# Slot tables of their own for the two batch entries, and the token chain's last norm on ScalarE, in a one-core vision block

## The reference

```python
# token stage: three 5-row convolutions over tokens x joints, a layer norm before each and one behind
h = layernorm(x, ln0_g, ln0_b); h = relu(conv2d(h, conv1_w, conv1_b, ((2, 2), (1, 1))))
h = layernorm(h, ln0_g, ln0_b); h = relu(conv2d(h, conv2_w, conv2_b, ((2, 2), (0, 0))))
h = layernorm(h, ln1_g, ln1_b); h = relu(conv2d(h, conv3_w, conv3_b, ((2, 2), (0, 0))))
h = layernorm(concat(h[:, :t], h[:, t:]), ln1_g, ln1_b) @ out_w + out_b
# attention with L1 distances, 8 heads of 64, a zero score added to each softmax
a[s, t, head] = -sum_w |q[s, head, w] - k[t, head, w]| / 8
a = softmax(concat(a, 0), axis=s)[:, :t]
o = sum over heads of (a applied to vf, and a transposed applied to vb)
h = h + x' + (o * sigmoid(1.702 * o)) @ fanin_w.T + fanin_b      # x' = layernorm(h)
# 32 experts, one chosen per token by argmax of x'' @ router_w.T
h = h + x'' + relu(relu(x'' @ W1[e] + b1[e]) @ W2[e] + b2[e])     # x'' = layernorm(h)
```

## Time and profile before

| | us |
|---|---|
| median of 3 runs | 3578.32 |
| lowest and highest | 3576.53, 3587.60 |
| the profiled execution's own time | 3586.24 |
| its span, first to last instruction | 3584.1 |

### The profile page before, as it was taken

How to read it: one execution, slowest core, us unless ns; L and a number is a source line. 1 busy time by engine, 2 the same in 40 slices (tenths; PEclk the granted TensorE clock), 3 DMA queues, 4 the chain that set the end, 5 groups by cost and what they waited for, 6 DMA issues and landing times. The chain is left out here.

```text
span 3584.1 us, 78481 instructions
## 1 busy us (share of the span) xinstructions
PE 3276.2 (91%) x23008; PEld 2420.3 (68%) x23008; DVE 3115.8 (87%) x4449; ACT 2694.5 (75%) x4801; POOL 2851.3 (80%) x2724
## 2 busy tenths in 40 slices
PE   5899999999999999999999999999999999999886
PEld 4666667666667766667666677666677666677554
DVE  3889988898898898888899899899899899898884
ACT  1777877777877777777777777777777777777774
POOL 1788888888888888878888888888888888888874
PEclk8999999999999999999999999999999999999998
DMA  3777877787777787777887777787877787777874
GB/s 94 154 157 153 161 151 154 150 165 154 156 153 156 153 162 156 155 148 151 158 160 155 157 153 154 157 158 155 159 153 155 156 158 155 155 153 152 160 157 82
DMA packets 198692, 545.31 MB, mean 152 GB/s; under 512 B 68054, under 2 KB 132438, under 8 KB 145272
## 3 DMA queue, kind: packets, MB, share of 16 engines
q0 software_dynamic: 73728, 503.35, 71.0%
q1 hardware_dynamic: 124920, 41.40, 5.9%
HBM read 10.79 MB, written 2.10 MB: 4 GB/s over the span
## 5 line engine op out<-in xcount | busy, mean ns | idle before, releaser
L805 DVE TENSOR_REDUCE S<-psU 128x16 f32<-128x1024 f32 x2176 | 2603.5, 1217 | 295.7 <-PE psU L403 288.4
L403 PE MATMUL psU<-flat,kT 99*128 99x256 bf16 x16384 | 2315.7, 275 | 230.5 <-ACT absd L601 106.6
L601 ACT ACTIVATE absd<-psU 128x1024 f32<-128x1024 f32 x1920 | 1957.8, 1023 | 627.0 <-PE psU L403 604.7
L403 PEld LDWEIGHTS psU<-flat,kT 99*128 99x128 bf16 x16384 | 1489.2, 98 | 915.2 <-DVE S L805 235.7
L1072 POOL TENSOR_TENSOR absd<-absd 128x1024 f32<-128x1024 f32 (+2 forms) x512 | 1182.1, 2309 | 195.3 <-DMA absd<-absd 194.3
L1061 POOL DMA_DIRECT2D absd<-absd x512 | 453.9, 886 | 297.6 <-ACT absd L601 254.5
L1076 POOL TENSOR_TENSOR absd<-absd 128x512 f32<-128x512 f32 (+2 forms) x512 | 611.0, 1193 | 40.2
L1079 POOL TENSOR_TENSOR absd<-absd 128x256 f32<-128x256 f32 (+2 forms) x512 | 352.4, 688 | 40.1
L415 PE MATMUL psC<-c1in,w 128*128 128x384 f32 (+1 forms) x930 | 315.1, 421 | 0.6
L501 PE MATMUL psZ<-P,v 128*128 128x256 f32 x1024 | 311.2, 386 | 0.8 <-ACT P L719 0.8
L434 PE MATMUL psC<-c3in,w 128*128 128x128 f32 x1240 | 255.6, 289 | 4.5 <-DVE c3in L847 4.2
(11 more groups left out here) (166 smaller groups left out, 2187.0 us busy)
## 6 DMA issues: line engine op xcount, KB each, us to landing
absd<-absd POOLq DMA_DIRECT2D x416, 1024.0 KB, 7.8
flat<-qparts SPq DMA_DIRECT2D x3072, 8.0 KB, 4.0
absd<-absd POOLq DMA_DIRECT2D x64, 768.0 KB, 6.5
absd<-absd POOLq DMA_DIRECT2D x32, 512.0 KB, 4.8
xin<-in_x SPq DMA_DIRECT2D x32, 192.0 KB, 7.9
flat<-pattern SPq DMA_DIRECT2D x4, 768.0 KB, 10.8
out_h<-result SPq DMA_DIRECT2D x32, 64.0 KB, 5.9
w<-in_w SPq DMA_DIRECT2D x1, 1280.0 KB
```

Of the source, the lines that this page charges most:

```text
L403: mm = nc.tensor.matmul(psU[:, slot % PLACES, m], kT[0:ROWS + 3, b, m, :], flat[0:ROWS + 3, half % HALVES, :, lo:lo + BLOCK], start=True, ...
L601: nc.scalar.activation(absd[:, c % GROUPS, :, u], psU[:, slot % PLACES].rearrange("p (n a) s w -> p n (a s w)", n=2), ACT.Abs).then_inc(a_ ...
L805: nc.vector.tensor_reduce(S[:, b, hd, SB * c:SB * c + SB], psU[:, slot % PLACES].rearrange("p a s w -> p s a w"), AX.XY, ALU.add, apply_ab ...
```

## The change

Three things are done. SHARED changes in two chunks: the third one's heads for ScalarE are (1, 2, 3, 4) instead of (0, 2, 4, 6), the fifteenth one's (2, 4, 6) instead of (0, 3, 6); the number of slices for each engine stays the same. LAST_AFTER goes from 17 to 21, and the tables KQ_AT and AT_AT become pairs of tables, one for each batch entry, with nearly all entries of all tables chosen anew; where the code read AT_AT["x"] it now reads AT_AT[b]["x"]. And the last norm of the token chain is applied on ScalarE as scale * x + bias, for which GpSimd makes the bias -mean * rstd by two more instructions (shift) behind the root, instead of VectorE's (x - mean) * rstd.

```diff
-SHARED = [(0, 2, 4, 6), (0, 2, 4, 6), (0, 2, 4, 6), (0, 2, 4, 6), (1, 3, 5), (0, 2, 4, 6), (0, 2, 4, 6), (0, 2, 4, 6),
-          (0, 2, 4, 6), (0, 2, 4, 6), (0, 2, 4, 6), (3, 6), (0, 2, 4, 6), (0, 2, 4, 6), (0, 3, 6), (0, 2, 4, 6)]
+SHARED = [(0, 2, 4, 6), (0, 2, 4, 6), (1, 2, 3, 4), (0, 2, 4, 6), (1, 3, 5), (0, 2, 4, 6), (0, 2, 4, 6), (0, 2, 4, 6),
+          (0, 2, 4, 6), (0, 2, 4, 6), (0, 2, 4, 6), (3, 6), (0, 2, 4, 6), (0, 2, 4, 6), (2, 4, 6), (0, 2, 4, 6)]
-LAST_AFTER = 17
+LAST_AFTER = 21
-TOK_ACT = Steps("copy relu1 relu2 relu3a relu3b turned")
+TOK_ACT = Steps("copy relu1 relu2 relu3a relu3b norm0 norm1 turned")
-TOK_DVE = Steps("".join(LN.format(x) + LN_APPLY.format(x) for x in "abc") + LN.format("d") + "norm0 norm1 h")
-TOK_POOL = Steps("vara rstda varb rstdb varc rstdc vard rstdd")
+TOK_DVE = Steps("".join(LN.format(x) + LN_APPLY.format(x) for x in "abc") + LN.format("d") + "h")
+TOK_POOL = Steps("vara rstda varb rstdb varc rstdc vard rstdd meand shiftd")
-KQ_AT = dict(kT=21, q=13, q_len=1, qpart1=13, qrest1=14, qpart2=38, qpart3=37)
-AT_AT = dict(vf=0, vb=7, v_len=0, turn_len=0, exp=20, exp_len=8, rden=27, scale=30, scale_len=8, turna=42, turnb=45,
-             pv=47, pv_len=8, half=52, sum=53, tanh=54, gate=58)
+KQ0 = dict(kT=22, q=13, q_len=0, qpart1=12, qrest1=13, qpart2=29, qpart3=37)
+KQ1 = dict(kT=15, q=11, q_len=1, qpart1=11, qrest1=13, qpart2=35, qpart3=32)
+KQ_AT = (KQ0, KQ1)
+AT0 = dict(vf=1, vb=7, v_len=0, turn_len=1, exp=20, exp_len=11, rden=32, scale=34, scale_len=7, turna=42, turnb=45,
+           pv=47, pv_len=7, half=52, sum=53, tanh=54, gate=55)
+AT1 = dict(vf=3, vb=6, v_len=0, turn_len=0, exp=20, exp_len=5, rden=27, scale=29, scale_len=13, turna=42, turnb=45,
+           pv=47, pv_len=5, half=52, sum=53, tanh=55, gate=56)
+AT_AT = (AT0, AT1)
-EX_AT = dict(fan=60, h2=59, rstd=58, x=67, turn=70, route=75, pick=76, turnoh=82, hida=84, hidb=86, hid_len=0, out=90,
-             out_len=4, back=105)
-NORM_AT = dict(stat=4, rstd=2, x=6, turn=38, part1=28, rest1=28, part2=32, part3=31, hx=89)
-HAND_AT = dict(xT=12, hx=65)
-TOK_AT = dict(copy=0, a=10, conv1=21, len1=22, b=45, conv2=55, len2=10, c=65, conv3=75, len3=32, d=108, turn=122,
-              out=126, root=0, gap=7)
+EX_AT = dict(fan=60, h2=59, rstd=64, x=67, turn=69, route=75, pick=75, turnoh=82, hida=85, hidb=87, hid_len=0, out=91,
+             out_len=5, back=105)
+NORM_AT = dict(stat=4, rstd=4, x=6, turn=36, part1=29, rest1=26, part2=33, part3=34, hx=87)
+HAND_AT = dict(xT=6, hx=89)
+TOK_AT = dict(copy=0, a=10, conv1=21, len1=22, b=44, conv2=55, len2=10, c=65, conv3=75, len3=30, d=108, turn=122,
+              out=125, root=0, gap=6)
...
                 if slot == TOK_AT["turn"]:
-                    pe.wait_ge(by_dve, TOK_DVE.after(q, "norm1"))
+                    pe.wait_ge(by_act, TOK_ACT.after(q, "norm1"))
...
+                if slot == TOK_AT["d"] + TOK_AT["gap"]:
+                    act.wait_ge(by_pool, TOK_POOL.after(q, "shiftd"))
...
+                    for b in range(2):
+                        nc.scalar.activation(resn[:, b, :], z[:, b * 2 * J:(b + 1) * 2 * J], ACT.Identity,
+                                             bias=nmr["d"][:, b:b + 1], scale=rstd["d"][:, b:b + 1]).then_inc(by_act, 1)
...
-                if slot == TOK_AT["d"] + TOK_AT["gap"]:
-                    dve.wait_ge(by_pool, TOK_POOL.after(q, "rstdd"))
-                    lead("turn")
-                    for b in range(2):
-                        nc.vector.tensor_scalar(resn[:, b, :], rows(2 * J)[:, b, :], mv["d"][:, b, 0:1],
-                                                rstd["d"][:, b:b + 1], ALU.subtract, ALU.mult).then_inc(by_dve, 1)
...
+                        if name == "d":
+                            shift("d", by_pool, lambda s: TOK_POOL.after(q, s + "d"))
```

More of the change, by code:

```diff
@@ L190, in vit_tower @@
         rstd = {k: sb("rstd" + k, [T, 2]) for k in "abcdne"}
-        mr = {k: sb("mr" + k, [T, 2]) for k in "ne"}
-        nmr = {k: sb("nmr" + k, [T, 2]) for k in "ne"}
+        mr = {k: sb("mr" + k, [T, 2]) for k in "dne"}
+        nmr = {k: sb("nmr" + k, [T, 2]) for k in "dne"}
         h = sb("h", [T, 2, LAT])
@@ L459, in kq @@
                 g = 2 * p + b
-                if slot == KQ_AT["kT"]:
+                if slot == KQ_AT[b]["kT"]:
                     take_bank(keys_act, K_ACT.after(g, "kT"))
@@ L467, in kq @@
                     mm.then_inc(keys_pe, 1)
-                for m in spread(slot, KQ_AT["q"], KQ_AT["q_len"], 2):
+                for m in spread(slot, KQ_AT[b]["q"], KQ_AT[b]["q_len"], 2):
                     if m == 0:
@@ L479, in attend @@
                 for n, name in enumerate(("vf", "vb")):
-                    for m in spread(slot, AT_AT[name], AT_AT["v_len"], 2):
+                    for m in spread(slot, AT_AT[b][name], AT_AT[b]["v_len"], 2):
                         if m == 0:
@@ L489, in attend @@
                 for n, name in enumerate(("turna", "turnb")):
-                    for m in spread(slot, AT_AT[name], AT_AT["turn_len"], 4):
+                    for m in spread(slot, AT_AT[b][name], AT_AT[b]["turn_len"], 4):
                         if m == 0:
@@ L496, in attend @@
                             mm.then_inc(at_pe, 1)
-                for n in spread(slot, AT_AT["pv"], AT_AT["pv_len"], HEADS):
+                for n in spread(slot, AT_AT[b]["pv"], AT_AT[b]["pv_len"], HEADS):
                     if n == 0:
@@ L624, in tok @@
                         nc.scalar.activation(y, y, ACT.Relu, bias=b3[:, hf:hf + 1]).then_inc(by_act, 1)
+                if slot == TOK_AT["d"] + TOK_AT["gap"]:
+                    act.wait_ge(by_pool, TOK_POOL.after(q, "shiftd"))
+                    if isinstance(p, int) and p == 1:
+                        act.wait_ge(lead_pe, TOK_PE.after(0, "turn"))
+                    for b in range(2):
+                        nc.scalar.activation(resn[:, b, :], z[:, b * 2 * J:(b + 1) * 2 * J], ACT.Identity,
+                                             bias=nmr["d"][:, b:b + 1], scale=rstd["d"][:, b:b + 1]).then_inc(by_act, 1)
                 if slot == TOK_AT["turn"] + 1:
@@ L678, in kq @@
                 g = 2 * p + b
-                if slot == KQ_AT["kT"] + 1:
+                if slot == KQ_AT[b]["kT"] + 1:
                     act.wait_ge(keys_pe, K_PE.after(g, "kT"))
@@ L685, in kq @@
                                          psZb[0:ROWS, 0:BLOCKS * T], ACT.Copy).then_inc(keys_act, 1)
[L686 removed]
+                if slot == KQ_AT[b]["qpart1"]:
                     act.wait_ge(queries_pe, Q_PE.after(g, "q"))
@@ L699, in attend @@
                 for n, name in enumerate(("vf", "vb")):
-                    if slot == AT_AT[name] + AT_AT["v_len"]:
+                    if slot == AT_AT[b][name] + AT_AT[b]["v_len"]:
                         act.wait_ge(at_pe, AT_PE.after(g, name))
@@ L703, in attend @@
                                              ACT.Copy).then_inc(at_act, 1)
-                for n in spread(slot, AT_AT["exp"], AT_AT["exp_len"], HEADS):
+                for n in spread(slot, AT_AT[b]["exp"], AT_AT[b]["exp_len"], HEADS):
                     if n == 0:
@@ L711, in attend @@
                                          accum_out=den[:, n:n + 1]).then_inc(at_act, 1)
-                for n in spread(slot, AT_AT["scale"], AT_AT["scale_len"], HEADS):
+                for n in spread(slot, AT_AT[b]["scale"], AT_AT[b]["scale_len"], HEADS):
                     if n == 0:
@@ L720, in attend @@
                                              psZ[:, :].rearrange("p (h t) -> p h t", h=4), ACT.Copy).then_inc(at_act, 1)
-                if slot == AT_AT["half"]:
+                if slot == AT_AT[b]["half"]:
                     act.wait_ge(at_pe, AT_PE.after(g, "pv"))
@@ L907, in kq @@
                 g = 2 * p + b
-                if slot == KQ_AT["qrest1"]:
+                if slot == KQ_AT[b]["qrest1"]:
                     dve.wait_ge(queries_act, Q_ACT.after(g, "qpart1"))
@@ L916, in attend @@
                 g = 2 * p + b
-                if slot == AT_AT["rden"]:
+                if slot == AT_AT[b]["rden"]:
                     dve.wait_ge(at_act, AT_ACT.after(g, "exp7"))
                     nc.vector.reciprocal(rden[:, :], den[:, :]).then_inc(at_dve, 1)
-                if slot == AT_AT["sum"]:
+                if slot == AT_AT[b]["sum"]:
                     dve.wait_ge(at_act, AT_ACT.after(g, "half"))
@@ L923, in attend @@
                         .then_inc(at_dve, 1)
-                if slot == AT_AT["gate"]:
+                if slot == AT_AT[b]["gate"]:
                     dve.wait_ge(at_act, AT_ACT.after(g, "tanh"))
@@ L1134, in kq @@
                 g = 2 * p + b
-                if slot == KQ_AT["qpart3"]:
+                if slot == KQ_AT[b]["qpart3"]:
                     pool.wait_ge(queries_act, Q_ACT.after(g, "qpart2"))
```

15 lines of the change are left out of this document (9 added, 6 removed).

## The result

The changed kernel takes 3792.98 us (median of six runs, 3788.12 to 3799.30) where the kernel before takes 3578.71 us (six runs, 3571.75 to 3587.60): 1.0595 times as long, 95% interval 1.0579 to 1.0611. The forecast was 3505, the range ended at 3568. Not only the size was wrong but the sign.

A forecast was written before the change was run, and what follows sets the result against it. No engine was full overall; losses of order in stretches where none was full bound it. Gains of 0.8 + 0 + 1.2 + 0.4 = 2.4 us, 31 times, plus 1 us prologue, gave 3512.8, median-adjusted 3505 us; range 3478 to 3568.

The forecast's parts named there:

- the norm of the token chain: Slot 114: two norm instructions leave VectorE (0.64 us) for ScalarE, 473 ns each, about 0.8 us, hidden in its idle time.
- the slower rival: Ring of four absd groups: ScalarE's first slices wait for later last sums; 50 us slower, 3628 us; chance 0.06.
- Slots 0 to 27: Start of the iteration: earlier v and x1T_late, and four ScalarE slices in a row, gain 0.8 us.
- rival (3): The run of four ScalarE slices starves VectorE, or slot numbers never set the order: 3575 us; chance 0.09.
- Slots 27 to 65: TensorE is full and the sum of its work stays the same: gain 0.
- Slots 65 to 84: Last sums four slots later no longer wait for GpSimd's tree: gain 0.55 us up to slot 84.
- the roots' new order: On GpSimd, slots 65 to 84: one DMA issue moves ahead of the expert norm's, hidden behind its DMA wait.
- Slots 84 to 97: Hidden products at slots 85 and 87 give ScalarE's one-hot copies a slot more: 0.8 us gained on TensorE's path.
- Slots 97 to 113: All is full, and the reciprocal and one more last sum come in: 0.15 us lost.
- Slots 113 to 128: The last pv matmul comes a slot earlier and two norm instructions go to ScalarE: gain 0.4 us.
- rival (1): Only plainly seen waits go (tree 0.54, pv 0.40 us an iteration), other gains becoming idle time: 3549 us; chance 0.20.
- rival (2): Only removed work counts, not order: VectorE loses 0.64 us an iteration, 20 us in all, 3558 us; chance 0.07.

The follow-up runs named there:

- e3: The changed kernel with 40 increments of an unused semaphore ahead of ScalarE's loop: 3566.26 us, ratio 0.9932 to the kernel before.
- e1: The kernel before with only the token chain's last norm moved to ScalarE, old tables kept: 3709.81 us, ratio 1.0333.
- e6: The kernel before with 5 idle instructions ahead of ScalarE's loop: 3587.14 us in one run.
- e4: The kernel before with ten increments of an unused semaphore ahead of ScalarE's loop: 3713.22 us, ratio 1.0345.
- s2: e3 with pv_len for entry 1 back at 8 instead of 5: 3552.80 us in one run.
- e2: The changed kernel with the token chain's last norm left on VectorE (new SHARED, tables and LAST_AFTER): 3571.39 us, ratio 0.9961.
- e5: The kernel before with 30 idle instructions ahead of ScalarE's loop: 3825.16 us in one run.

## Why the prediction was wrong

**The step that failed** is the one on the norm of the token chain: "come to ScalarE at slot 114", with 473 ns each and "in cover". As work this was right: the two instructions take 455 ns each in e3 and 456 in the changed kernel, inside the signs given, and in e1, which has this part alone, slots 113 to 128 take 12.38 us against 12.36: they are hidden. What was left out is that instructions also take up room: three more in the loop and seven ahead of it push its end from 439 to 449, over the border that lies between (e6, e4). What the runs showed in its place is a pause of 4.27 us at each of 28 branches, and 9.06 us more in each iteration, where the step had put nothing. No term of the sum and none of the four rivals held this; the slower rival, the ring of absd, did not occur (no wait of ScalarE's slices for a last sum in any trace). Could it have been seen? The trace of before shows the loop's 281 instructions, no pause, and an instruction queue with 20 packets, but not where the border is: neither the pause nor its price could be read from it.

**The price** has two parts. In the old order (e4) the iteration grows from 107.68 to 112.56 us, 4.88: slots 0 to 8 add 4.35 and slots 11 to 16 1.02, and the others give a little back; 4.05 is the longer pause. In the new order it grows from 107.22 (e3) to 116.28, 9.06, with a pause that is longer by 4.06. The difference between the two orders, 4.2 us an iteration, is thus not the pause; it goes with the clock. Windows of e4 at slots 0 to 3, 3 to 8, 8 to 16 and 16 to 27:

```profile
520.59:525.74 5.15, 2.35 (x16) 1.77 (x17) 2.73 (x4) 1.08 (x2) 4.01 (x4) 0.97 0.73 144
525.74:531.79 6.05, 6.05 (x24) 4.04 (x25) 4.35 (x8) 4.50 (x7) 2.79 (x8) 0.50 0.36 72
531.79:538.20 6.41, 6.41 (x37) 4.66 (x36) 4.27 (x8) 4.57 (x7) 5.44 (x6) 0.70 0.85 170
538.20:548.15 9.95, 8.61 (x60) 5.81 (x59) 9.48 (x13) 7.96 (x20) 6.71 (x6) 1.00 0.70 146
```

In e4 TensorE's granted clock is 0.50 for 10.24 us of this iteration, and in the changed kernel for 20.48 of the one shown above; over the run that is 407 against 603 us (123 before). Slots 0 to 8 and 11 to 16 hold most of the 9.06: 12.14 and 6.84 us in the changed kernel, 6.14 and 4.53 in e3. Why the lower level lasts twice as long in the new order wasn't tried and stays open; in both TensorE had been busy for less than half of slots 0 to 3 (1.66 of 4.50 and 2.35 of 5.15 us).

**The terms of the order**, from e3:
- Slots 0 to 27, 0.8 forecast: 0.87 measured. VectorE goes from slot 15 to slot 27 in 9.43 us (9.35 forecast), with 0.22 us of idle time behind the run of four, so rival (3) did not occur. The method, following places by hand from rows, was right here.
- Slots 27 to 65, 0 forecast: 0.46 lost. The argument "it is full, and the sum is the same" excludes a gain; it doesn't exclude a loss. TensorE is idle for 0.18 of 31.75 us before and for 0.44 of 32.21 in e3: with its products in a heap it is less full, and s2, which spreads them again, gets 0.39 back.
- Slots 65 to 84, 0.55 forecast: 0.20 lost. The waits of the last sums went as foreseen, from 33.0 us and 44 times to 12.4 and 4. But the roots' new order was costed at nothing, with a wait of GpSimd's as cover, and the wait came back one step on, as VectorE's wait for rstdc (21.2 us, 31 times).
- Slots 84 to 97, 0.8 forecast: 0.29 lost. The idle time of VectorE before slot 85, 1.37 us in the earlier trace rows, is gone in e3, as foreseen. It stands before slot 95 now:

```profile
1454.67 1.23 DVE L821 TENSOR_REDUCE S<-psU 128x16 f32<-128x1024 f32 x1 [1.62 <-PE psU L409]
```

  At slot 91 e3 is 1.16 us ahead of before, counted from slot 84 (6.54 against 7.70), and at slot 97 0.29 behind: the hidden and output products were moved later by a slot each, not removed, and TensorE does them all in this stretch. I took a head start for a gain.
- Slots 97 to 113, 0.15 loss forecast: 0.19 gained. Slots 113 to 128, 0.4 forecast: 0.17. The waits of o_half fell from 83.6 us to 17.6, far more than the 20 asked for. But only 28 us of this fall are this stretch's, where each wait went from 1.24 to 0.36 us, and they bought less than half of what was counted. The other 38 are entry 1's, from pv_len 5, in slots 27 to 65, which got longer; they are back in s2, which is faster. The line of e3 and that of s2:

```profile
ACT o_half L739 <- PE psZ L507: 17.6, 33, 6.2
ACT o_half L739 <- PE psZ L507: 55.8, 64, 5.5
```

The sum is a gain of 0.46 us an iteration by the medians of whole iterations, and 0.27 by the stretches, instead of 2.4: 8 to 14 us over 31. The timed ratio of e3 gives 15 to 33. The spans of the two profiled executions differ by 16.7: 13.1 over the 31 iterations, of which 3.9 in the first, 1.7 ahead of it and 1.8 behind the last of them, so the medians leave out the gain at the two ends. Without the pause the changed kernel would stand at 0.9932 x 3578 = 3554, inside the range, between rival (1)'s 3549 and rival (2)'s 3558. That would have been luck: of the six stretches only the first came out near its size, and three came out with the other sign. The mechanism of rival (1), a gain in one stretch that is idle time in the next, is what slots 65 to 97 show.

Rival (2), that only removed work counts, is refuted by e1 and e4, which have the pause: in e1 VectorE lacks the two instructions (it is busy for 3110.9 us, in e4 for 3122.7), the pauses are 4.11 and 4.25 us, and the iterations are equal within 0.02 us. Without a pause e2 and e3, in the same new order, differ by the norm: 3571.39 and 3566.26 us, 5 of the rival's 20, with ratios whose intervals overlap. (Rival (3) is mis-added by 3 us: stretch one at -0.8 and half of 1.2 and of 0.4 make 0, so 3578 and not 3575. Nothing here hangs on it.) Taking this work off VectorE gained nothing that is clear of noise, though rival (2) had it as the fullest engine by what it holds.

Of the signs, the period (105.6), slots 27 to 65 and the wait for GpSimd failed; TensorE's wait at slot 11 (0.54 us in e3, under 1), VectorE from 15 to 27, o_half, slot 85 and resn's duration held. Those that held were signs of single steps, and these steps did happen; none of them watched the whole of the stretch in which its step stood.

## What to carry to other kernels

The instructions of ScalarE's loop had a place as well as a duration here: the same 284 paused for 4.27 us a turn from 165 on and for 0.21 from 205 on. So when even a few are added to an engine's loop, or ahead of it, count that engine's list before and after, and after the change look for an "issue" gap behind the branch and for packets in the instruction queue. A pause of one engine was paid again by TensorE's clock here (0.50 for 603 us of the changed kernel's run, for 112 of e3's), so that 40 idle instructions ahead of the loop were worth 227 of 3793 us. When steps are moved in a stretch where an engine is full, read the stretch to its end: idle time that vanishes at one slot counts only if no other slot takes it up.

## What the runs showed of the hardware

- ScalarE's taken branch cost 0.2 us in the runs whose loop touches two blocks and 3.6 to 4.3 us where it touches three, by the borders found above (191, and between 443 and 449). Ten instructions that do nothing moved the time by 127 us (e4, 3713.22 against 3586.56), and five by nothing that is clear of noise (e6, 3587.14; before, 3573.47 to 3591.43).
- With the border three instructions behind the loop's start a second pause of 4.34 us follows (e5); with the border 23 or 26 behind it (e4, after) there is none. Nothing between 3 and 23 was tried, and why the two differ isn't shown.
- After each such pause TensorE's granted clock was 0.50 for 10.2 to 21.9 us of slots 0 to 20 in e4 and in the changed kernel, in all of 28 iterations (10.2 in 24 of them in e4, 17.1 and more in 24 of them in the changed kernel); before, this happened in one of 28.
